# Layer 0's neighbour sum of the next batch as three fp32r products instead of fp32 ones, in a pipelined four-layer GNN kernel

## The reference

```python
# x 32x512x256, adj 32x512x512 (zero off the diagonal but for some 1.6% of the places,
# values 0.05 to 1), nodemask 32x512, all float32; heads of 32
def reference(x, adj, nodemask, ...):
    # layer 0: neighbour sum, then a feed-forward block of width 1024
    h = relu(layernorm(x))
    agg = epsilon * h + einsum('bnm,bmd->bnd', adj, h)
    u = agg @ W1 + b1
    u = silu(u * rsqrt(mean(u * u) + 1e-6) * rms_weight)
    x = x + u @ W2 + b2
    # layer 1: additive attention
    h = relu(layernorm(x)); g = h @ W.T + b
    att = sigmoid((g @ a1)[:, :, None] + (g @ a2)[:, None, :] + att_b) * adj  # and node masks
    x = x + (att / (att.sum(-1) + 1e-8)) @ g
    # layer 2: eight heads, softmax where adj != 0
    h = relu(layernorm(x))
    x = x + softmax(q @ k.T / sqrt(32) + adj * W_e[head]) @ v @ W_o.T
    # layer 3: normalized graph convolution
    h = relu(layernorm(x)); d = (adj.sum(-1) + 1e-5) ** -0.5
    return x + (d[:, :, None] * adj * d[:, None, :]) @ (h @ weight) + bias
```

## Time and profile before

| | before |
|---|---|
| three runs | 3564.43, 3564.73, 3568.19 us, median 3564.73 |
| the profiled execution | 3567.06 us; its span 3565.2 us, so 1.9 us lie around it |
| mean granted TensorE clock | 0.994 |
| busy | TensorE 3447.6 us (97%), VectorE 2655.7 (74%), ScalarE 2286.7 (64%), GpSimd 943.1 (26%) |
| one pass of the loop | 108.7 us from store to store (1514.46 to 1623.18, 1732.02 after it) |
| load of `adjT_f` | issued at 1599.20 in the pass shown, 5.2 us to landing |
| ScalarE between layer 3's two roundings (`a_hi`) | idle from 1609.60 to 1615.27 |
| the first values, 12 matmuls of 256 columns | from 1631.66 on, 0.12 us each |
| first hidden tile | GpSimd's three steps on its squares 1632.62 to 1633.71, VectorE's first use of them at 1635.79 |

### The profile page before, as it was taken

The page is one execution under the profiler, slowest core; times in us unless marked ns, Lnnn a source line. Parts: engine busy times, 40 slices in busy tenths (PEclk is TensorE's granted clock), DMA queues, the critical chain, the costliest instruction groups (busy, mean ns, idle before and its releaser), DMA issues.

```text
span 3565.2 us, 70163 instructions
## 1 busy us (share of the span) xinstructions
PE 3447.6 (97%) x19886; PEld 2560.3 (72%) x20108; DVE 2655.7 (74%) x6794; ACT 2286.7 (64%) x5062; POOL 943.1 (26%) x2379
## 2 busy tenths in 40 slices
PE   6999999999999999999999999999999999999997
PEld 4777777777777777777777777777777777777774
DVE  6777777777787777777777877777777778777774
ACT  4666666666676666666666776666766667766664
POOL 2222331222322223322223212233222232122320
PEclk8999999999999999999999999999999999999999
DMA  3233223232232332232322223322323222323212
GB/s 102 50 94 90 76 65 88 59 95 74 73 83 64 84 94 71 65 95 53 95 77 74 79 71 77 95 71 71 89 53 95 81 75 75 76 72 95 71 54 65
DMA packets 166941, 275.09 MB, mean 77 GB/s; under 512 B 23908, under 2 KB 59876, under 8 KB 166760
## 3 DMA queue, kind: packets, MB, share of 16 engines
q1 hardware_dynamic: 164200, 269.25, 28.3%
q10 hardware_dynamic: 2560, 4.20, 0.6%
HBM read 122.37 MB, written 16.78 MB: 39 GB/s over the span
## 4 chain that ended last, share of the span: by engine, by line
PE 76%; issue 8%; ACT 7%; DVE 4%; DMA 3%; SPq 2%; DVEq 0%; POOL 0%; ACTq 0%; POOLq 0%
PE turn L1361 10%; PE value L1376 7%; PE score L1403 6%; PE front L1256 6%; PE front L1192 6%; PE score L1352 6%; PE front L1162 5%; PE front L1164 5%; PE front L1163 5%; ACT prob L646 3%; PE score L1349 3%; PE front L1219 2%; DMA qk_stack<-qk 2%; ACT pT L655 2%; PE score L1393 2%
## 5 line engine op out<-in xcount | busy, mean ns | idle before, releaser
L646 ACT ACTIVATE prob<-prob,small 128x512 f32<-128x512 f32 x1024 | 737.5, 720 | 351.7 <-DVE small L1001 344.3
L1001 DVE CUSTOM_DVE_ANT_0 prob<-score,adj_sb,drv 128x512 f32<-128x512 f32 x1024 | 759.2, 746 | 192.7 <-PE score L1352 184.7
L1361 PE MATMUL turn<-ident,prob 128*128 128x128 f32 x4096 | 626.1, 275 | 50.7 <-ACT prob L646 45.1
L1352 PE MATMUL score<-qk_stack 128*128 128x512 f32 x1024 | 592.2, 582 | 21.8 <-DMA qk_stack<-qk 21.7
L1361 PEld LDWEIGHTS turn<-ident,prob 128*128 128x128 f32 x4096 | 479.7, 141 | 181.4 <-issue 64.8
L655 ACT ACTIVATE pT<-turn 128x512 f32<-128x512 f32 x768 | 449.0, 585 | 72.5 <-PE turn L1361 42.3
L449 POOL TENSOR_TENSOR small<-small 128x1 f32<-128x1 f32 x128 | 24.9, 195 | 1401.2 <-ACT aside L580 1401.2
L758 DVE TENSOR_TENSOR s_lo<-front,s_hi 128x512 fp32r<-128x512 f32 x316 | 216.7, 686 | 151.5 <-ACT s_hi L539 151.5
L1349 PE MATMUL score<-unlinked,neg_mask 128*128 128x512 bf16 x802 | 306.1, 382 | 0.3 <-DVE small L1001 0.3
L1162 PE MATMUL front<-w_hi,s_hi 128*128 128x256 f32 x1024 | 300.6, 294 | 0.8 <-DVE w_lo L758 0.8
L1163 PE MATMUL front<-w_lo,s_hi 128*128 128x256 f32 x1024 | 288.3, 282 | 0.0
(11 more groups left out here) (209 smaller groups left out, 7871.6 us busy)
## 6 DMA issues: line engine op xcount, KB each, us to landing
qk_stack<-qk SPq DMA_DIRECT2D x992, 128.0 KB, 2.4
adjT_f<-in_adjT SPq DMA_DIRECT2D x32, 1024.0 KB, 5.2
adj_sb<-in_adj SPq DMA_DIRECT2D x32, 1024.0 KB, 7.5
prob<-in_adjT SPq DMA_DIRECT2D x32, 1024.0 KB, 5.3
x_new<-in_x SPq DMA_DIRECT2D x32, 512.0 KB, 4.2
out<-x_out SPq DMA_DIRECT2D x32, 512.0 KB, 3.0
qk_stack<-qk ACTq DMA_DIRECT2D x32, 128.0 KB, 2.6
pT<-in_W SPq DMA_DIRECT2D x2, 1024.0 KB, 10.9
```

Source lines behind the costliest of these rows:

```text
L646: act.activation(prob[:, i % 8, :], prob[:, i % 8, :], ACT.Exp, bias=nmax[:, h, n:n + 1], scale=-1.0, accum_out=prsum[:, h, n:n + 1]).then ...
L1001: dve.tensor_tensor_reduce(out=prob[:, i % 8, :], in0=SB_[i % 2][:, :], in1=adj_sb[:, n, :], scale=neg_w[:, h:h + 1], scalar=3e38, op0=ALU ...
L1352: pe.matmul(SB_[i % 2][:, :], qk_stack[:, h % 4, 0, tile(n)], qk_stack[:, h % 4, 1, :], start=False, stop=True).then_inc(sc_ps, 1)
L1361: last = pe.transpose(TB[k % 2][:, tile(n)], prob[:, (4 * h + n) % 8, tile(j)], ident[:, :])
```

## The change

Layer 0's sum of the next batch is now split in three products. ScalarE rounds the rows and the adjacency (`h_hi` 128x1024, `af_hi` 128x2048), VectorE subtracts (`af_lo` in two halves of 128x1024, then `h_lo` 128x1024, "rows' low part last"). TensorE runs `aggregate_high` (8 fp32r matmuls of 512 columns) where `aggregate(nx, 0)` was, then `project3` and `turn` in swapped order, then `aggregate_low` (16 matmuls) where `aggregate(nx, 1)` was. Both sums are finished together, so both `aggregated` move to the end. VectorE's `diagonal` moves between the two `attended1`, and `update3` is split: tile 0 ahead of `turned`, the rest behind it. In the head, `project_v(t, 0)` and ScalarE's `values(t, 0)` go ahead of the hidden products and their squares. Batch 0's own sum stays as it was.

```diff
--- before.py
+++ after.py
@@ -117,6 +117,10 @@
         wl_stage = region[:, 5632:6144].rearrange("p (k n) -> p k n", k=DT)
         w3_stage = region[:, 5120:5632].rearrange("p (k n) -> p k n", k=DT)
         msg = region[:, 5120:6144].rearrange("p (n d) -> p n d", n=NT)
+        af_hi = sb("af_hi", [P, NT, N], F32R, over="pT")
+        af_lo = sb("af_lo", [P, NT, N], F32R, over="pT", skip=4 * 2048)
+        h_lo = sb("h_lo", [P, NT, D], F32R, over="pT", skip=4 * 4096)
+        h_hi = sb("h_hi", [P, NT, D], F32R, over="pT", skip=4 * 7168)
         inv_x = sb("inv_x", [P, NT, HG, HD], over="hb")
         small = sb("small", [P, 236])
 
@@ -560,6 +566,16 @@
             def norm0(tf):
                 layernorm(tf, 0, f_norm, norm_tiles(0), x_new, h0)
 
+            def rows_high(nx):
+                act.wait_ge(f_norm["ready"], at(nx, 8, 4))
+                hi(h_hi[:, :, :], h0).then_inc(h_hi_ready, 1)
+
+            def adjacency_high(nx):
+                act.wait_ge(diag_eps, at(nx, 1, 1))
+
+                act.wait_ge(att_added, at(nx, 3, 0))
+                hi(af_hi[:, :, :], adjT_f[:, :, :]).then_inc(af_hi_ready, 1)
+
             def aggregated(tf, d):
                 act.wait_ge(agg_ps, at(tf, 2, d + 1))
                 hi(T_hi[:, d, :], FB[d][:, :]).then_inc(T_hi_ready, 1)
@@ -674,11 +690,10 @@
                     qk_high(t, 0, 0)
                     qk_high(t, 0, 1)
                     stack_high(t)
+                    values(t, 0)
                 if f:
                     square(tf, 0, 0)
                     square(tf, 0, 1)
-                if b:
-                    values(t, 0)
                 for g in GRID:
                     if g in prepare:
                         prepare[g]()
@@ -720,16 +735,18 @@
                     attended1(tf, 1)
                 if nx is not None:
                     norm0(nx)
+                    rows_high(nx)
                 if b:
                     gathered(t, 0)
+                if nx is not None:
+                    adjacency_high(nx)
+                if b:
                     gathered(t, 1)
                 if f:
                     layernorm(tf, 0, b_norm, norm_tiles(50), x2, hf)
+                    turned(tf)
                 if nx is not None:
                     aggregated(nx, 0)
-                if f:
-                    turned(tf)
-                if nx is not None:
                     aggregated(nx, 1)
 
             norm0(0)
@@ -859,6 +876,18 @@
             def aggregated(tf, d):
                 dve.wait_ge(T_hi_ready, at(tf, 2, d + 1))
                 lo(T_lo[:, d, :], FB[d][:, :], T_hi[:, d, :]).then_inc(T_lo_ready, 1)
+
+            def rows_low(nx):
+
+                dve.wait_ge(h_hi_ready, at(nx, 1, 0))
+                lo(h_lo[:, :, :], h0, h_hi[:, :, :]).then_inc(h_lo_ready, 1)
+
+            def adjacency_low(nx):
+
+                dve.wait_ge(b_norm["normed"], at(nx, 5, -1))
+                dve.wait_ge(af_hi_ready, at(nx, 1, 0))
+                for m in (slice(0, 2), slice(2, 4)):
+                    lo(af_lo[:, m, :], adjT_f[:, m, :], af_hi[:, m, :]).then_inc(af_lo_ready, 1)
 
             def restore_diagonal(tf):
                 dve.wait_ge(diag_eps, at(tf, 1, 1))
@@ -1042,10 +1071,11 @@
                 dve.wait_ge(agg3_hi, at(t, 2, d + 1))
                 lo(a3_lo[:, d, :], SB_[d][:, :], a3_hi[:, d, :]).then_inc(agg3_lo, 1)
 
-            def update3(t):
-                dve.wait_ge(b3_added, at(t, 1, 1))
-                dve.wait_ge(dinv_ready, at(t, 1, 1))
-                for n in range(NT):
+            def update3(t, which):
+                if which[0] == 0:
+                    dve.wait_ge(b3_added, at(t, 1, 1))
+                    dve.wait_ge(dinv_ready, at(t, 1, 1))
+                for n in which:
                     dve.wait_ge(proj3_ps, at(t, 4, n + 1))
                     dve.scalar_tensor_tensor(out=x_out[:, n, :], in0=proj3_bank(n), scalar=dinv[:, n:n + 1],
                                              in1=x_out[:, n, :], op0=ALU.mult, op1=ALU.add).then_inc(out_ready, 1)
@@ -1116,23 +1146,27 @@
                     stats0(nx)
                 if f:
                     attended1(tf, 0)
-                    attended1(tf, 1)
-                    factors1(tf)
                 if nx is not None:
                     diagonal(nx)
                 if f:
+                    attended1(tf, 1)
+                    factors1(tf)
                     update1(tf)
                 if b:
                     gathered(t, 0)
                     gathered(t, 1)
                 if nx is not None:
-                    aggregated(nx, 0)
+                    adjacency_low(nx)
+                    rows_low(nx)
+                if b:
+                    update3(t, (0,))
                 if f:
                     turned(tf)
                 if b:
-                    update3(t)
+                    update3(t, (1, 2, 3))
 
             def next_aggregate(nx):
+                aggregated(nx, 0)
                 aggregated(nx, 1)
                 restore_diagonal(nx)
 
@@ -1192,6 +1226,28 @@
                     last = pe.matmul(FB[d][:, :], h0[:, m, tile(d)], adjT_f[:, m, :], start=(m == 0), stop=(m == NT - 1))
                 last.then_inc(agg_ps, 1)
 
+            def aggregate_high(nx):
+
+                pe.wait_ge(h_hi_ready, at(nx, 1, 0))
+                pe.wait_ge(af_hi_ready, at(nx, 1, 0))
+                pe.wait_ge(msg_ready, at(nx, 4, 0))
+                for d in range(DT):
+                    for m in range(NT):
+                        pe.matmul(FB[d][:, :], h_hi[:, m, tile(d)], af_hi[:, m, :], start=(m == 0), stop=False)
+
+            def aggregate_low(nx):
+
+                for m in range(NT):
+                    if m % 2 == 0:
+                        pe.wait_ge(af_lo_ready, at(nx, 2, m // 2 - 1))
+                    for d in range(DT):
+                        pe.matmul(FB[d][:, :], h_hi[:, m, tile(d)], af_lo[:, m, :], start=False, stop=False)
+                pe.wait_ge(h_lo_ready, at(nx, 1, 0))
+                for d in range(DT):
+                    for m in range(NT):
+                        last = pe.matmul(FB[d][:, :], h_lo[:, m, tile(d)], af_hi[:, m, :], start=False, stop=(m == NT - 1))
+                    last.then_inc(agg_ps, 1)
+
             def hidden(tf, n, c):
                 if isinstance(tf, int) and tf == 0:
                     if n > 1:
@@ -1428,11 +1484,11 @@
                 if b:
                     project_qk(t, 0, 0)
                     project_qk(t, 0, 1)
+                if b:
+                    project_v(t, 0)
                 if f:
                     hidden(tf, 0, 0)
                     hidden(tf, 0, 1)
-                if b:
-                    project_v(t, 0)
                 if shared is not None:
                     shared()
                 for g in GRID:
@@ -1483,15 +1539,15 @@
                 if b:
                     aggregate3(t, 1)
                 if nx is not None:
-                    aggregate(nx, 0)
+                    aggregate_high(nx)
                 if shared is not None:
                     pe.wait_ge(setup_dve, SETUP_DVE)
+                if b:
+                    project3(t, tf)
                 if f:
                     turn(tf)
-                if b:
-                    project3(t, tf)
                 if nx is not None:
-                    aggregate(nx, 1)
+                    aggregate_low(nx)
 
             pe.wait_ge(setup_dve, 7)
             aggregate(0, 0)
```

More of the change, by code:

```diff
@@ L170, in gnn_kernel @@
         table_in = sem("table_in")
+        h_hi_ready, h_lo_ready, af_hi_ready, af_lo_ready = (
+            sem(n) for n in ("h_hi_ready", "h_lo_ready", "af_hi_ready", "af_lo_ready"))
         unlinked_ready, deg_ready = sem("unlinked_ready"), sem("deg_ready")
```

## The result

| | before | after |
|---|---|---|
| median of six runs each | 3564.81 us | 3580.74 us |
| range | 3564.27 to 3568.19 | 3579.27 to 3582.82 |
| ratio of the medians, 95% interval | | 1.0042 (1.0031 to 1.0052) |
| profiled execution, its span | 3567.06, 3565.2 us | 3580.11, 3578.3 us |

What follows compares the result with a forecast made beforehand. TensorE, holding 76% of the chain, was taken as the bound. On the profiled 3567.06 us: -37.5 (TensorE) + 37.5 (wait on the store) + 4 = 3571, or 3569 by the median; range 3532 to 3598.

Steps and rivals of the forecast that it cites:

- in turns: Likeliest case, chance 0.42: VectorE's subtractions and GpSimd's add_b2 alternate on the SBUF port; 3569 us, own range 3558 to 3582.
- within 0.2%: Outcome forecast as the same: a measurement can tell about 0.2%, 7 us, from no change.
- The turns: VectorE's three subtractions against GpSimd's add_b2: each turn costs 1.66 us, third subtraction ends at 1622.05.
- The open question of that step: Whether GpSimd slips in between two of VectorE's back-to-back instructions; no row showed it, taking turns was assumed.
- The store's tie: x_out's store releases qk_high 3.04 us after issue, first score 5.62 later; TensorE stands about 1.9 us.
- TensorE's saving: Two fp32 halves of 6.86 us become 24 fp32r matmuls of 5.61: 1.25 us a pass, -37.5 us over 30.
- Moved steps at 0: Moving diagonal and putting values first were each taken as 0; diagonal's possible gain was 0 to 1.2 us.
- The added 4 us: Store-to-score chain read in a quiet batch may run longer in normal passes: 0.15 us x 30 = 4 us.
- The clock: Rival, chance 0.12: TensorE's wait lowers its clock; one pass in three +13, 3582 us, or half price each pass, 3608.
- The sign set down for it: A granted clock under 0.98 over the span would show the clock's rival.
- The rivals on the fast side: TensorE's saving arrives: VectorE keeps the port, chance 0.22, 3536 to 3541 us; or little disturbance, chance 0.10, 3527.

Runs made afterwards that it cites:

- e5: Changed kernel with x_out moved from over qk to over prob and VectorE's loop head placed elsewhere; 3527.68 us, ratio 0.9910.
- e9: e5 with the first values back behind the first hidden products on TensorE, and ScalarE's copy behind the squares; 3527.37 us, ratio 0.9892.
- e10: e5 with VectorE's diagonal back behind layer 1's factors; 3526.72 us, ratio 0.9888.
- e7: Kernel before with three unused VectorE subtractions ahead of each loop pass's last x_out, TensorE's work untouched; 3609.30 us, ratio 1.0123.
- e8: Changed kernel with fp32 products kept, roundings and subtractions unused, transposes ahead of project3, first half sum announced when done; 3580.92 us, ratio 1.0043.
- e2: Changed kernel with GpSimd's add_b2 held back until h_lo is written, behind the three subtractions; 3571.38 us, ratio 1.0016.
- e1: Changed kernel with x_out moved from over qk to over prob, so qk_high no longer waits for the store; 3539.13 us, ratio 0.9922.
- e4: Changed kernel with all its roundings, subtractions and moves, but TensorE keeps the fp32 products and uses none of them; 3619.58 us, ratio 1.0144.
- e3: Changed kernel with both x_out moved over prob and add_b2 held back until h_lo is written; 3567.30 us, ratio 1.0006.
- e6: e3 with VectorE's loop head placed as in e5; 3526.08 us, ratio 0.9886.
- e11: Changed kernel with only VectorE's loop head placed as in e5, x_out staying over qk; 3582.02 us, ratio 1.0044.

## Why the prediction came out as it did

The likeliest case, "in turns", was the right mechanism, and 3580.7 lies in the range of 3532 to 3598; but the time is 12 us above the 3569 forecast, and "within 0.2%" became slower.

- **The turns** were right to 0.1 us. The forecast had 1.66 us a turn and the third subtraction ending 5.05 us after `normed`; measured are (1735.99 - 1732.62) / 2 = 1.69 a turn and 1735.99 + 1.76 = 1737.75, 5.17 after 1732.39 + 0.19. GpSimd's additions stretched to 5.78 us instead of "over 6". The open question of that step, whether GpSimd slips in between VectorE's back-to-back instructions, is answered: it does, each time.
- **The store's tie** was right: `qk_high` waits for the store in every pass, 8.68 us from its issue to the score (8.66), TensorE waits 1.78 us (about 1.9).
- **TensorE's saving** of 1.25 us was right, and it was given back in full; e5 shows it as 1.29.
- **Moved steps at 0**: right (e9, e10).
- **The added 4 us** failed in size: 0.15 us x 30 was a guess from a quiet batch, and it measured 0.21 x 29 = 6.1. From `normed` to the first score the forecast had 16.75 us and 16.87 is measured, the turns' last tenth; the other tenth is the pass of before that it was held against, 16.74 where the loop's mean is 16.63.
- **The clock** is the step that failed: it was left out of the sum of the likeliest case, and stood as a rival with a chance of 0.12, "one pass in three" at 1.3 us each. It came in 8 of 29 passes at 1.0: 8 us of the 14. I had read that the wait would be shorter than the last batch's and left it there; e7 shows that such a wait alone brings the lower clock, e8 that 0.7 us does not. The rival's 3582 is nearly the measured time. The sign set down for it, a granted clock under 0.98 over the span, was wrong by the prediction's own price: eight such stretches moved it from 0.994 to 0.992. With both terms put right the sum is 3567.06 - 37.5 + 37.5 + 6.1 + 8.0 - 1.2 (the first and the last two rows of the table) = 3580.0, the profiled 3580.1; the new terms are read from that same execution, so this says where the time is and tests nothing.
- **The rivals on the fast side** (3527, and 3536 to 3541) missed a limit: even with the port free (e2) or the store away (e1), VectorE's late instructions at the loop's top held the pass. In the kernel before, VectorE stood there anyway for ScalarE's `T_hi` (3.52 us), which hid the jump. I gave the moved `T_lo` no price because I looked at what releases them and not at when VectorE can issue them.

Open: what picks the passes that get the lower clock. It followed 8 of 29 waits of 1.6 us and more here, 8 of 21 in e4, 6 of 13 in e3, 2 of 17 in e2 and 2 of 20 in e7, and these are no longer than the ones that it didn't follow. The spread of e2's executions and their clocks suggests that the number changes from one execution to the next; only one of each kernel was profiled. Open too: how the late instructions of VectorE and the store act on each other. In e3 and e2 most passes have either the second `T_lo` 3.0 us behind the first and the store landing in 3.7, or 3.4 us and 3.3; without the late instructions (e6) the store takes 3.0.

## What to carry to other kernels

A saving on the bounding engine that is paid with work on a second one has to pass every tie of the second engine's tail: here a store out of a tile that the next pass writes took all of it. Before giving up such a change, take the tie away: an `x_out` in another tile and a loop head in another place turned +0.4% into -1.1%. And where a wait of TensorE grows in every pass, put a price on its clock too, not only on the wait: here 1.0 us in some quarter of the passes.

## What the runs showed of the hardware

- VectorE and GpSimd, both reading two SBUF operands, alternated strictly: 128x1024 subtractions went from 1.22 to 1.76 us, 128x256 additions from 0.74 to 1.72.
- A wait of 1.74 to 1.86 us of TensorE, once a pass, was followed by 3.4 us at the lower clock in 8 of 29 passes (about 1.0 us each) in the changed kernel. In the other profiled executions the lower clock inside the loop came only behind waits of 1.61 us and more (e2, e3, e4, e7, e11), in 2 to 8 passes; no shorter one was followed by it, so none in e1 (up to 0.94 us) and e8 (up to 1.27).
- VectorE's queue took 3.1 us from the loop's branch to its first step, others 0.2 to 0.3, and a second gap of 1.7 to 2.4 us followed; putting the loop's head at the start of a block of its program took both away.
